# A decoder block on one core: cross attention scores from joined key halves, and maxima added by one product per bank

## The chip, the cores and the metric

The program runs on one core of one Trainium2 chip. The metric is the device time of one execution in microseconds (us). A core has five engines that run side by side, each with its own queue: PE (TensorE, matrix products into the eight PSUM banks), DVE (VectorE), ACT (ScalarE), POOL (GpSimd) and SP (SyncE, which here only issues DMAs). They wait for one another through semaphores. "PEld" in the profile is TensorE's loading of a stationary operand.

## The reference, cut to what matters

A decoder block over 64 sequences of 128 tokens, width 256, float32: a local attention, a cross attention on a second input (`ctx_1024`), and a slot network, each behind a layer norm and added to x. The change lies in the cross attention, 16 heads of 16:

```python
q = relu(query @ Wq + bq); k = relu(key @ Wk + bk); v = relu(value @ Wv + bv)
scores = einsum('bqhd,bkhd->bhqk', qh, kh) / sqrt(16)
scores = where(causal, scores, NEG)
probs = softmax(scores, axis=-1)
out = einsum('bhqk,bkhd->bqhd', probs, vh) + q
return layer_norm(out, gamma, beta)
```

## The kernel before, in words

Three stages follow one another: the local attention (to about 882 us of the profiled execution), the cross attention (882 to 1478 us) and the slot network. x stays in SBUF. A step works on a pair of sequences (`at`, 32 pairs); `tt` is the sequence in the pair. Each engine has its own program of steps in which `prev` is the pair one step behind, `old` two and `older` three; `pairs` (line 79) writes out the first and last steps and loops over the rest with two steps in a loop body. The order inside a step is written out by hand for each engine (`step`, TensorE's at line 1513), and no planner reorders it.

**Layout of the heads.** Queries and keys lie with the head dimension on the partitions: two projections (`e` = 0, 1) of 128 rows each. A row group `i` of 32 partitions (`group`, 1434) holds two heads, 16 rows each. To give each head its own product over 32 rows, `evac_k` (1567) writes the keys twice, once with the rows of one head made zero and once with the other's (`half`). A head's product has a stationary operand of 32 rows by 128 columns and a moving one of 32 rows by 128 columns; in float32 the trace shows two passes (two instructions) per product. The four row groups write the four score banks, group `i` bank `i`, and their products run beside one another. `slot(i, j)` is the j-th 128 columns of bank i.

**Per sequence**, TensorE does the following:
- `scores` (1440): 16 mask products (1453, bfloat16, 32x32 tiles, 512 columns), then 16 products query by key (1459) with the queries stationary, so that rows are queries. VectorE's `row_max` (1680) reduces all 16 heads at once, and `max_parts` (1684) splits the negated maximum into two bfloat16 parts and writes them to `max_part`, in 128 columns of which 32 are used.
- `max_transpose` (1464): one bfloat16 transpose of `max_part` into a bank; ScalarE's `copy_max` (1600) copies 128 columns to `max_t`.
- `scores_t` (1473): 16 products key by query (1482), keys stationary, so that rows are keys; after the four products of a `j` come four products (1485, bfloat16, 128 columns) with the stationary operand `pick` that add the negated maxima of slot (i, j). For tt = 1 the first product of a bank waits for ScalarE's exponential of that bank of tt = 0 (`exp_done`). The wait for `max_t` stands ahead of all of them.
- ScalarE's `exp` (1606), POOL's causal mask `mask_weights` (1786), and TensorE's `values` (1489), `back` (1503).

**Order around the change.** TensorE's step: scores(prev,0), back(old,0), values(old,1), project_k 0, scores(prev,1), max_transpose(prev,0), back(old,1), project_k 1, project_q 0, scores_t(prev,0), project_q 1, project_v 0, max_transpose(prev,1), scores_t(prev,1), project_v 1, transpose_q, transpose_x, values(prev,0), transpose_ctx. ScalarE's (1619): evac_av(old,1), copy_max(prev,0), evac_k, exp(prev,0), copy_max(prev,1), evac_q, exp(prev,1), copy_q_tok, relu_v, copy_xn, evac_av(prev,0), copy_ctx. VectorE's is at 1723, POOL's at 1810: mask_weights(old,1), scale_normed, add_query, mask_weights(prev,0), then the two pairs of reciprocal-deviation operations (`one_over_deviation`, 1774), which wait for VectorE's `sum_moments` and `x_moments`; these stand behind `bias_v` (1693), which waits for `project_v`.

Of the kernel before, what the change touches and what calls it, by code (L numbers as in the profile page):

```python
# [6 lines left out]
BF16 = mybir.dt.bfloat16  # L7
# [12 lines left out]
PT = 2 * S  # L20
# [138 lines left out]
class CrossWeights:  # L159


    def __init__(self, nc, scope):
        def sb(name, shape, dt=F32):
            return scope.enter_context(nc.sbuf_tensor(name, shape, dt))

        self.w_qk = sb("w_qk_b", [128, C, 4, 128])
        self.b_qk = sb("b_qk_b", [128, 4])
        self.w_v = sb("w_v_b", [128, C, D])
        self.b_v = sb("b_v_b", [128, D])
        self.gamma = sb("gamma", [128, D])  # L170
        self.beta = sb("beta", [128, D])
        self.mask = sb("mask_b", [128, 4, 128], BF16)
        self.row_half = sb("row_half", [128, 2])
        self.b_k = sb("b_k_half", [128, 2, 2])
        self.pick_f = sb("pick_f", [128, 4])
        self.pick = sb("pick", [128, 4, 128], BF16)
        self.minus_half = sb("minus_half", [128, 2])
        self.eps = sb("eps", [128, 2])


def attentions(nc, scope, sem, a, bank, x_sb, ident, ident_bf, cross):
# [87 lines left out]
    with nc.Block() as block:  # L269
# [39 lines left out]
        def _(dve):  # L309
# [25 lines left out]
            for w, g, products in terms:  # L335
# [9 lines left out]
            nc.vector.tensor_reduce(cross.pick_f[:],  # L345
                                    ident[:].rearrange("p (i u j) -> p j u i", i=4, j=4)[:, :, 0:2, :], AX.XY,
                                    ALU.add).then_inc(cross_made, 1)
# [8 lines left out]
            nc.vector.tensor_copy(cross.pick[:], cross.pick_f[:].unsqueeze(2).to_broadcast([128, 4, 128])  # L356
                                  ).then_inc(cross_made, 1)
            dve.wait_ge(cross_made, 5)
# [932 lines left out]
def cross_attention(nc, scope, sem, a, score_banks, bank, x_sb, ident, ident_bf, cross, slot_weights):  # L1291
# [6 lines left out]

    def sb(name, shape, dt=F32):
        return scope.enter_context(nc.sbuf_tensor("c_" + name, shape, dt))  # L1300
# [17 lines left out]
    k_z = [[sb(f"k_z{i}_{half}", [128, 2, PT]) for half in range(2)] for i in range(2)]  # L1318
# [4 lines left out]
    max_part = sb("max_part", [128, 2, 128], BF16)  # L1323
    max_t = sb("max_t", [128, 2, 128], BF16)
# [37 lines left out]
    with nc.Block() as block:  # L1362
# [19 lines left out]
        def _(pe):  # L1382
# [57 lines left out]
            def scores(at, tt):  # L1440
                if tt == 0:
                    pe.wait_ge(q_ready, at.count(1, 1))
                    pe.wait_ge(k_ready, at.count(1, 1))
                else:
                    pe.wait_ge(max_done, at.count(2, 1))
                    pe.sem_inc(pe_turn, 1)
                for i in range(4):
                    if tt == 0:
                        wait(pe, exp_done, at.count(8, i - 3))
                        pe.sem_inc(pe_turn, 1)  # L1450
                    for c in range(4):
                        rows = group((i + c) % 4)
                        pe.matmul(score_banks[group(c), i, :].rearrange("p (j k) -> p j k", j=4), ident_bf[rows, rows],
                                  cross.mask[rows, c, :].unsqueeze(1).to_broadcast([32, 4, 128]),
                                  start=True, stop=False, skip_group_check=True)
                toks = slice(S * tt, S * tt + S)
                for j in range(4):
                    for i in range(4):
                        mm = pe.matmul(slot(i, j), q_f[at.par][group(i), j % 2, toks],  # L1459
                                       k_z[at.par][j // 2][group(i), j % 2, toks],  # L1460
                                       start=False, stop=(j == 3), skip_group_check=True)
                mm.then_inc(sc_filled, 1)

            def max_transpose(at, tt):
# [3 lines left out]
                else:  # L1468
                    pe.wait_ge(maxT_ready, at.count(2, 1))
                pe.transpose(maxT_bank[:].bitcast(BF16)[:, 0:128], max_part[:, tt, :],  # L1470
                             ident_bf[:]).then_inc(maxT_filled, 1)

            def scores_t(at, tt):
                if tt == 0:
                    pe.wait_ge(max_done, at.count(2, 2))
                pe.wait_ge(maxT_ready, at.count(2, tt + 1))
                toks = slice(S * tt, S * tt + S)
                for j in range(4):
                    for i in range(4):
                        if tt == 1 and j == 0:  # L1480
                            pe.wait_ge(exp_done, at.count(8, i + 1))
                        pe.matmul(slot(i, j), k_z[at.par][j // 2][group(i), j % 2, toks],  # L1482
                                  q_f[at.par][group(i), j % 2, toks], start=True, stop=False, skip_group_check=True)
                    for i in range(4):
                        mm = pe.matmul(slot(i, j), cross.pick[group(i), j, :], max_t[group(i), tt, :],  # L1485
                                       start=False, stop=True, skip_group_check=True)
                mm.then_inc(sct_filled, 1)

            def values(at, tt):
# [5 lines left out]
                for h in range(H):  # L1495
                    g, j = h // 4, h % 4
                    if j == 0:
                        pe.wait_ge(masked, at.count(8, 4 * tt + g + 1))
                    mm = pe.matmul(av_bank[HW * j:HW * j + HW, 128 * g:128 * g + 128], v_heads[at.par][:, tt, h, :],  # L1499
                                   probs_t[tt][:, h, :], start=True, stop=True, skip_group_check=True)  # L1500
# [53 lines left out]
        def _(act):  # L1554
# [12 lines left out]
            def evac_k(at):  # L1567
                act.wait_ge(k_filled, at.count(2, 2))
                wait(act, sct_filled, at.count(2, -2))
                for half in range(2):  # L1570
                    for e in range(2):
                        ins = nc.scalar.activation(k_z[at.par][half][:, e, :], k_bank[:, e * PT:e * PT + PT], ACT.Relu,  # L1572
# [27 lines left out]
            def copy_max(at, tt):  # L1600
                act.wait_ge(maxT_filled, at.count(2, tt + 1))
                wait(act, sct_filled, at.count(2, tt - 1))
                nc.scalar.activation(max_t[:, tt, :], maxT_bank[:].bitcast(BF16)[:, 0:128],  # L1603
# [45 lines left out]
        def _(dve):  # L1649
# [34 lines left out]
            def max_parts(at, tt):  # L1684
                dve.wait_ge(max_done, at.count(2, tt + 1))
                wait(dve, maxT_filled, at.count(2, tt - 1))
                parts = max_part[:, tt, :].rearrange("p (i u j) -> p u i j", i=4, j=4)
# [704 lines left out]
```

## Time and profile before

| | us |
|---|---|
| median of 3 runs | 1788.61 (1787.81 to 1790.47) |
| the profiled execution's own time | 1789.42 |
| its span, first to last instruction | 1787.0 |
| cross attention in it | about 882 to 1478 |
| TensorE busy, whole span | 1612.1 (90%) |
| VectorE, ScalarE, POOL busy | 1367.5 (77%), 967.2 (54%), 946.1 (53%) |

The profiled execution took 2.42 us more than its span and lies 0.81 us above the median. Busy TensorE time counts from an instruction's start to a modelled end, so neighbours overlap: for throughput, read the distance between starts, not the durations. A row's "[0.44 <-ACT c_max_t L1603]" says that the engine stood idle 0.44 us before it and which instruction released it.

### The profile page before, as it was taken

To read this page: it belongs to the slowest core of one execution; us is meant where nothing else is said; L and a number is where in the kernel's file an instruction comes from. 1 tells how busy PE (TensorE), PEld (TensorE's weight loads), DVE (VectorE), ACT (ScalarE), POOL (GpSimd) and SP (SyncE) were. 2 spreads that over 40 slices of the span, in tenths; PEclk is the share of its full clock that TensorE was granted. 3 is DMA by queue.
4 is the path that set the end of the run, shared out by engine and by line. 5 is a ranking of instruction groups with operands and counts; after the bars stand their busy time and mean duration, and the time that the engine had idled before them with its cause. 6 is when DMAs were issued, how large, how long until landed. Compare 5 with 4: busy or idle time off the path is not lost. (4 is left out here: it accounts for less than half of the span.)

```text
span 1787.0 us, 52814 instructions
## 1 busy us (share of the span) xinstructions
PE 1612.1 (90%) x18272; PEld 1162.9 (65%) x18334; DVE 1367.5 (77%) x3280; ACT 967.2 (54%) x2049; POOL 946.1 (53%) x1205
## 2 busy tenths in 40 slices
PE   2799999999999999999699999999999976999997
PEld 1566666666666666666477777777777754666664
DVE  4688898989898989898356666666666644898996
ACT  1355555554555555555256565656565633777774
POOL 2345454545555555554336666666666662445544
PEclk9899999999999999999799999999999976999998
DMA  5554455545554455444210000000000000001001
GB/s 102 81 85 87 84 84 84 88 82 83 84 90 82 80 85 91 82 73 80 72 45 14 18 12 18 12 18 12 18 12 18 7 2 1 25 30 35 29 29 41
DMA packets 124323, 92.64 MB, mean 52 GB/s; under 512 B 34849, under 2 KB 122850, under 8 KB 124258
## 3 DMA queue, kind: packets, MB, share of 16 engines
q1 hardware_dynamic: 124258, 91.80, 28.1%
q8 instruction: 38, 0.62, 0.2%
q14 instruction: 27, 0.22, 0.1%
HBM read 23.06 MB, written 8.39 MB: 18 GB/s over the span
## 5 line engine op out<-in xcount | busy, mean ns | idle before, releaser
L1205 POOL TENSOR_SCALAR_AFFINE_SELECT probs_t<-probs_t 128x512 f32<-128x512 f32 x256 | 186.5, 743 | 220.7 <-ACT probs_t L894 220.6
L1682 DVE TENSOR_REDUCE c_neg_max<-score_banks 128x16 f32<-128x2048 f32 x64 | 146.5, 2290 | 100.4 <-PE score_banks L1459 100.3
L1610 ACT ACTIVATE c_probs_t<-score_banks 128x512 f32<-128x512 f32 x256 | 132.2, 603 | 66.0 <-PE score_banks L1485 66.0
L1791 POOL TENSOR_SCALAR_AFFINE_SELECT c_probs_t<-c_probs_t 128x512 f32<-128x512 f32 x256 | 155.4, 643 | 11.8 <-ACT c_probs_t L1610 11.7
L564 PE MATMUL score_banks<-xn_t,w_qk_a 128*128 128x256 f32 x512 | 133.7, 395 | 0.7 <-ACT xn_t L803 0.7
L1482 PE MATMUL score_banks<-c_q_f,c_k_z 32*128 32x128 f32 x2048 | 106.4, 307 | 22.0 <-ACT c_max_t L1603 15.4
L1482 PEld LDWEIGHTS score_banks<-c_q_f,c_k_z 32*128 32x128 f32 x2048 | 92.1, 188 | 45.3 <-ACT c_probs_t L1610 20.1
L713 PE MATMUL bank<-probs_t,v_heads 128*32 128x128 f32 x2048 | 109.2, 285 | 2.7 <-POOL probs_t L1205 0.8
L1042 DVE TENSOR_REDUCE neg_max<-score_banks 128x4 f32<-128x512 f32 x128 | 87.6, 684 | 21.3 <-PE score_banks L625 21.2
L894 ACT ACTIVATE probs_t<-bank 128x512 f32<-128x512 f32 x128 | 76.1, 595 | 41.4 <-PE bank L700 41.3
L564 PEld LDWEIGHTS score_banks<-xn_t,w_qk_a 128*128 128x128 f32 x512 | 91.6, 194 | 10.0 <-ACT xn_t L803 1.1
L1802 POOL TENSOR_TENSOR c_scaled<-c_normed,gamma 128x512 f32<-128x512 f32 x32 | 40.7, 1271 | 97.2 <-DVE c_normed L1665 97.2
L894 ACT ACTIVATE probs_t<-score_banks 128x512 f32<-128x512 f32 x128 | 76.1, 594 | 26.1 <-PE score_banks L700 25.9
L1042 DVE TENSOR_REDUCE neg_max<-bank 128x4 f32<-128x512 f32 x128 | 87.7, 685 | 2.6 <-PE bank L625 1.0
L1696 DVE TENSOR_TENSOR c_v_raw<-bank,b_v_b 128x512 f32<-128x512 f32 x32 | 22.1, 691 | 87.8 <-PE bank L1421 77.9
L2294 POOL TENSOR_TENSOR r_hn<-rz_t,half_hn 128x256 f32<-128x256 f32 x32 | 23.4, 731 | 124.0 <-ACT rz_t L2126 124.0
L2063 PE MATMUL bank<-w_ih,gi_t 128*128 128x512 f32 (+1 forms) x256 | 88.4, 488 | 0.4 <-DVE n_in L2229 0.2
L599 PE MATMUL score_banks<-w_v_a,xn_t 128*128 128x336 f32 x256 | 87.4, 464 | 0.3 <-ACT lat_raw L848 0.3
L1616 ACT ACTIVATE c_av_t<-bank 128x512 f32<-128x512 f32 x64 | 40.0, 625 | 77.7 <-PE bank L1499 77.7
L1572 ACT ACTIVATE c_k_z<-bank,b_k_half,row_half 128x256 f32<-128x256 f32 x128 | 61.9, 564 | 33.1 <-PE bank L1403 33.1
L1016 DVE TENSOR_TENSOR qk_rest<-qk_f,qk_part 128x512 f32<-128x512 f32 x64 | 74.9, 1170 | 6.1 <-ACT qk_f L829 6.1
L1499 PE MATMUL bank<-c_probs_t,c_v_heads 128*32 128x128 f32 x2048 | 74.4, 281 | 2.5 <-POOL c_probs_t L1791 1.8
(266 smaller groups left out, 4692.9 us busy)
## 6 DMA issues: line engine op xcount, KB each, us to landing
q_stack<-qk_part SPq DMA_DIRECT2D x192, 128.0 KB, 3.5
k_stack<-qk_part SPq DMA_DIRECT2D x192, 128.0 KB, 4.6
c_ctx_in<-in_ctx SPq DMA_DIRECT2D x32, 256.0 KB, 2.7
out<-y SPq DMA_DIRECT2D x32, 256.0 KB, 2.1
x_sb<-in_x SPq DMA_DIRECT2D x30, 256.0 KB, 2.7
rq_stack<-lat_part SPq DMA_DIRECT2D x192, 32.0 KB, 2.3
rk_stack<-lat_part SPq DMA_DIRECT2D x192, 16.0 KB, 1.9
w_ih<-in_ffn_w_ih SPq DMA_DIRECT2D x1, 768.0 KB, 5.8
```

The lines of the kernel that those rows point to most:

```text
L564: mm = pe.matmul(dst, w(c), src[:, c, :], start=(c == 0), stop=(c == C - 1))
L599: mm = pe.matmul(v_bank[tt][:, 0:n], src[:, c, S * tt:S * tt + S], w_v[:, c, :], start=(c == 0), stop=(c == C - 1))
L713: mm = pe.matmul(av_bank[HW * j:HW * j + HW, 128 * (g % 4):128 * (g % 4) + 128], v_heads[at.par][:, tt, h0 + j, :], probs_t[g % 4][:, j, : ...
L894: nc.scalar.activation(probs_t[g % 4][:].rearrange("p j t -> p (j t)"), score_bank[g % 2][:], ACT.Exp, scale=SCALE).then_inc(exp_done, 1)
L1016: nc.vector.tensor_tensor(rest, src, part[0], ALU.subtract).then_inc(part_step, 1)
L1042: nc.vector.tensor_reduce(neg_max[:, tt, h0:h0 + 4], score_bank[g % 2][:].rearrange("p (j k) -> p j k", k=128), AX.X, ALU.max, negate=True ...
L1205: nc.gpsimd.affine_select(out=pt[:], in_=pt[:], pattern=[[0, 4], [1, 128]], compare_op=ALU.is_ge, fill=0.0, base=-1 if local else 0, chann ...
L1482: pe.matmul(slot(i, j), k_z[at.par][j // 2][group(i), j % 2, toks], q_f[at.par][group(i), j % 2, toks], start=True, stop=False, skip_group ...
L1610: nc.scalar.activation(probs_t[tt][:, 4 * g:4 * g + 4, :].rearrange("p j q -> p (j q)"), score_banks[:, g, :], ACT.Exp, scale=SCALE).then_ ...
L1682: nc.vector.tensor_reduce(neg_max[:, tt, :], all_scores, AX.X, ALU.max, negate=True).then_inc(max_done, 1)
L1791: nc.gpsimd.affine_select(out=heads, in_=heads, pattern=[[0, 4], [1, 128]], compare_op=ALU.is_ge, fill=0.0, base=0, channel_multiplier=-1) ...
L2063: mm = pe.matmul(gate_bank[b][:, 0:hi - lo], gi_t[:, c, :], w.w_ih[:, c, lo:hi], start=(c == 0), stop=(c == C - 1))
```

## The change

The keys of both halves move into one tile, `k_z[par][:, e, half, :]`. In `scores`, one product with the same stationary query block takes both halves as a moving operand of 256 columns (two stretches of 128), 8 products in place of 16. This makes slot (i, j) hold e = j // 2 and half = j % 2, where it was the other way round; `scores_t` and `values` follow (`slot_j`). `max_parts` spreads the parts over four blocks of 128 columns, one per slot; `max_transpose` transposes four blocks in place of one, and `copy_max` copies 512 columns. In `scores_t` the 16 products key by query come first, without the pick products between; then comes the wait for `max_t`, and one product of 512 columns per bank against a tile of ones adds the maxima of its four heads, 4 products in place of 16. `pick` and `pick_f` go, `ones` comes.

```diff
-        self.pick_f = sb("pick_f", [128, 4])
-        self.pick = sb("pick", [128, 4, 128], BF16)
+        self.ones = sb("ones_b", [128, 128], BF16)
...
-            nc.vector.tensor_reduce(cross.pick_f[:],
-                                    ident[:].rearrange("p (i u j) -> p j u i", i=4, j=4)[:, :, 0:2, :], AX.XY,
-                                    ALU.add).then_inc(cross_made, 1)
+            nc.vector.memset(cross.ones[:], 1.0).then_inc(cross_made, 1)
...
-            nc.vector.tensor_copy(cross.pick[:], cross.pick_f[:].unsqueeze(2).to_broadcast([128, 4, 128])
-                                  ).then_inc(cross_made, 1)
-            dve.wait_ge(cross_made, 5)
+            dve.wait_ge(cross_made, 4)
...
-    k_z = [[sb(f"k_z{i}_{half}", [128, 2, PT]) for half in range(2)] for i in range(2)]
+    k_z = [sb(f"k_z{i}", [128, 2, 2, PT]) for i in range(2)]
...
-    max_part = sb("max_part", [128, 2, 128], BF16)
-    max_t = sb("max_t", [128, 2, 128], BF16)
+    max_part = sb("max_part", [128, 2, 4, 128], BF16)
+    max_t = sb("max_t", [128, 2, 512], BF16)
...
-                for j in range(4):
+                for e in range(2):
                     for i in range(4):
-                        mm = pe.matmul(slot(i, j), q_f[at.par][group(i), j % 2, toks],
-                                       k_z[at.par][j // 2][group(i), j % 2, toks],
-                                       start=False, stop=(j == 3), skip_group_check=True)
+                        mm = pe.matmul(score_banks[:, i, 256 * e:256 * e + 256].rearrange("p (s k) -> p s k", s=2),
+                                       q_f[at.par][group(i), e, toks], k_z[at.par][group(i), e, :, toks],
+                                       start=False, stop=(e == 1), skip_group_check=True)
                 mm.then_inc(sc_filled, 1)
...
-                pe.transpose(maxT_bank[:].bitcast(BF16)[:, 0:128], max_part[:, tt, :],
-                             ident_bf[:]).then_inc(maxT_filled, 1)
+                for j in range(4):
+                    mm = pe.transpose(maxT_bank[:].bitcast(BF16)[:, 128 * j:128 * j + 128], max_part[:, tt, j, :],
+                                      ident_bf[:])
+                mm.then_inc(maxT_filled, 1)
...
-                pe.wait_ge(maxT_ready, at.count(2, tt + 1))
                 toks = slice(S * tt, S * tt + S)
                 for j in range(4):
                     for i in range(4):
                         if tt == 1 and j == 0:
                             pe.wait_ge(exp_done, at.count(8, i + 1))
-                        pe.matmul(slot(i, j), k_z[at.par][j // 2][group(i), j % 2, toks],
-                                  q_f[at.par][group(i), j % 2, toks], start=True, stop=False, skip_group_check=True)
-                    for i in range(4):
-                        mm = pe.matmul(slot(i, j), cross.pick[group(i), j, :], max_t[group(i), tt, :],
-                                       start=False, stop=True, skip_group_check=True)
+                        pe.matmul(slot(i, j), k_z[at.par][group(i), j // 2, j % 2, toks],
+                                  q_f[at.par][group(i), j // 2, toks], start=(j == 0), stop=False, skip_group_check=True)
+                pe.wait_ge(maxT_ready, at.count(2, tt + 1))
+                for i in range(4):
+                    mm = pe.matmul(score_banks[:, i, :], cross.ones[group(i), :], max_t[group(i), tt, :],
+                                   start=False, stop=True, skip_group_check=True)
                 mm.then_inc(sct_filled, 1)
...
-                                   probs_t[tt][:, h, :], start=True, stop=True, skip_group_check=True)
+                                   probs_t[tt][:, 4 * g + slot_j, :], start=True, stop=True, skip_group_check=True)
...
-                nc.scalar.activation(max_t[:, tt, :], maxT_bank[:].bitcast(BF16)[:, 0:128],
+                nc.scalar.activation(max_t[:, tt, :], maxT_bank[:].bitcast(BF16)[:, 0:512],
                                      ACT.Copy).then_inc(maxT_ready, 1)
...
-                parts = max_part[:, tt, :].rearrange("p (i u j) -> p u i j", i=4, j=4)
+                parts = max_part[:, tt, :, :].rearrange("p j (i u) -> p u i j", i=4)
```

## Rows read from the trace of the kernel before

**Rows 1.** The page: TensorE's busy time, its share of the span, instructions.

```profile
PE 1612.1 (90%) x18272; PEld 1162.9 (65%) x18334; DVE 1367.5 (77%) x3280; ACT 967.2 (54%) x2049; POOL 946.1 (53%) x1205
```

**Rows 2.** Busy time by engine over 29 steady steps (x: instructions).

```profile
936.00:1451.00 515.00, 495.33 (x8778) 386.76 (x8778) 335.81 (x717) 300.19 (x665) 335.13 (x460) 1.00 0.05 14
```

**Rows 3.** Line 1682, the row maxima: durations, first and last start.

```profile
L1682 DVE TENSOR_REDUCE c_neg_max<-score_banks x64: 2280/2292/2293, 898.8 to 1451.4; 128x16 f32<-128x2048 f32 x64
```

**Rows 4.** Waits, 930 to 1470 us: total us, times, longest us.

```profile
PEld score_banks L1482 <- ACT c_probs_t L1610: 20.1, 26, 0.8
...
PE score_banks L1482 <- ACT c_max_t L1603: 14.7, 30, 2.1
...
PEld bank L1499 <- POOL c_probs_t L1791: 7.0, 17, 0.4
```

**Rows 5.** Timeline of one step: start, length (us), engine, line [idle before].

```profile
1203.01 1.17 PE L1459 MATMUL score_banks<-c_k_z,c_q_f 32*128 32x128 f32 x32
...
1204.12 0.23 PE L1470 MATMUL bank<-ident_bf,c_max_part 128*128 128x128 bf16 x1
...
1204.41 2.28 DVE L1682 TENSOR_REDUCE c_neg_max<-score_banks 128x16 f32<-128x2048 f32 x1
...
1204.62 1.03 PE L1403 MATMUL bank<-c_ctx_t,w_qk_b 128*128 128x256 f32 x4
...
1205.49 1.03 PE L1403 MATMUL bank<-c_xn_t,w_qk_b 128*128 128x256 f32 x4
...
1206.75 0.50 PE L1482 MATMUL score_banks<-c_q_f,c_k_z 32*128 32x128 f32 x8 [0.23 <-DVE c_neg_max L1682]
...
1207.07 0.23 PE L1485 MATMUL score_banks<-c_max_t,pick 32*128 32x128 bf16 x4
...
1207.13 0.46 PE L1482 MATMUL score_banks<-c_q_f,c_k_z 32*128 32x128 f32 x8
...
1207.40 0.23 PE L1485 MATMUL score_banks<-c_max_t,pick 32*128 32x128 bf16 x4
...
1208.07 0.23 PE L1485 MATMUL score_banks<-c_max_t,pick 32*128 32x128 bf16 x4
...
1210.07 0.22 PE L1470 MATMUL bank<-ident_bf,c_max_part 128*128 128x128 bf16 x1
1210.32 0.28 ACT L1603 ACTIVATE c_max_t<-bank 128x128 bf16<-128x128 bf16 x1
...
1210.73 0.70 PE L1482 MATMUL score_banks<-c_q_f,c_k_z 32*128 32x128 f32 x6 [0.44 <-ACT c_max_t L1603]
...
1212.38 0.21 PE L1485 MATMUL score_banks<-c_max_t,pick 32*128 32x128 bf16 x1
...
1212.63 2.07 ACT L1610 ACTIVATE c_probs_t<-score_banks 128x512 f32<-128x512 f32 x4 [1.30 <-PE score_banks L1485]
...
1213.49 0.60 PE L1430 MATMUL bank<-ident,c_q_f 128*128 128x128 f32 x4
...
1213.93 0.60 PE L1388 MATMUL bank<-ident,c_xn 128*128 128x128 f32 x4
...
1216.67 2.40 POOL L1791 TENSOR_SCALAR_AFFINE_SELECT c_probs_t<-c_probs_t 128x512 f32<-128x512 f32 x4
```

**Rows 6.** Groups by line and form, 900 to 1500 us: busy us, mean ns | idle.

```profile
L1616 ACT ACTIVATE c_av_t<-bank 128x512 f32<-128x512 f32 x64 | 40.0, 625 | 77.7 <-PE bank L1499 77.7
...
L1453 PE MATMUL score_banks<-mask_b,ident_bf 32*32 32x512 bf16 x1008 | 32.1, 384 | 2.0 <-DVE c_neg_max L1682 2.0
...
L1603 ACT ACTIVATE c_max_t<-bank 128x128 bf16<-128x128 bf16 x64 | 17.8, 278 | 68.2 <-PE bank L1470 68.2
```

**Rows 7.** Timeline of the start of the cross attention.

```profile
884.31 0.17 DVE L1756 MEMSET c_max_part<- 128x128 uint32 x1
...
885.39 1.09 PE L1397 MATMUL bank<-ident,c_ctx_in 128*128 128x128 f32 x4 [4.33 <-DMA c_ctx_in<-in_ctx]
```

**Rows 8.** Timeline of vector engine's first work after the set-up block.

```profile
26.39 0.75 DVE L985 BATCH_NORM_STATS2 stats<-x_sb 128x6 f32<-128x256 f32 x2 [7.27 <-PEq L269]
```

More of the change, by code:

```diff
@@ L1496, in values @@
                     g, j = h // 4, h % 4
+                    slot_j = 2 * (j % 2) + j // 2
                     if j == 0:
@@ L1571, in evac_k @@
                     for e in range(2):
-                        ins = nc.scalar.activation(k_z[at.par][half][:, e, :], k_bank[:, e * PT:e * PT + PT], ACT.Relu,
+                        ins = nc.scalar.activation(k_z[at.par][:, e, half, :], k_bank[:, e * PT:e * PT + PT], ACT.Relu,
                                                    bias=cross.b_k[:, half, e:e + 1],
```

## The prediction

> **What bounds the kernel now.** I read the page first, then the busy time by engine of the cross attention, then its waits, then one step of the timeline. The page shows TensorE busy 90% of the span [rows 1]. The change touches only the cross attention, so its own table counts: over 29 steady steps of 515.0 us, 17.76 us a step, TensorE is busy 495.3 us, VectorE 335.8, POOL 335.1, ScalarE 300.2, at full granted clock (1.00, 2.4 GHz) [rows 2]. TensorE is the bound, with 0.68 us idle a step. The row maxima show how long the stage lasts: first start 898.8, last 1451.4, 64 of them [rows 3], for 32 steps.
>
> The waits say where the idle time lies: TensorE's products of `scores_t` wait 14.7 us, 30 times, about 0.5 us a step, for `max_t` (tt = 1; its weight loads, ahead of it, wait 20.1 us for the exponentials of tt = 0); POOL's mask holds `values` back 7.0 us in all, 17 times [rows 4]. The timeline shows the rest. `row_max` of tt = 1 runs from 1204.41 to 1206.69 while TensorE does transposes and two projections, and `scores_t` of tt = 0 starts at 1206.75 after 0.23 us of idle time; so that stretch is nearly balanced between VectorE and TensorE. `scores_t` of tt = 1 starts at 1210.73 after the 0.44 us wait, and lasts until 1212.59; `exp` follows at 1212.63 [rows 5]. A step's period is thus a path that is TensorE nearly everywhere, with short stretches handed to `row_max`, `exp` plus `copy_max`, and POOL.
>
> A difference within 0.2% (3.6 us) is about what a measurement of this kernel can't tell from none.
>
> **The change part by part**, per step of two sequences.
>
> *Joined key halves in `scores`.* Before, 32 passes of 128 columns take from 1203.01 to the next operation's start at 1204.12, 1.11 us; that is 8 passes in each of four row groups that run side by side, 0.139 us a pass. A pass of 256 columns over the whole array takes (1205.49 - 1204.62) / 4 = 0.218 us [rows 5], so doubling the columns costs less than double: some of the 128-column pass is the exchange of the stationary operand. After, 4 passes of 256 columns per row group are 0.87 us, and 0.97 if the 0.1 us of changing over to the next operation is in the 1.11. I take a saving of 0.14 us per sequence, with ends 0 (cost goes by columns) and 0.24. For tt = 1 it counts in full: `row_max` starts at its end. For tt = 0, TensorE next meets `values(old,1)`, which already waits for POOL in 17 of 30 steps [rows 4]; POOL's mask (1216.67, 2.40 us [rows 5]) follows from `project_v` through VectorE's and POOL's small operations and doesn't move with `scores`. I take 0.05.
>
> The Trainium skill (TensorE: Matmul & The Clock Gate, "Back-to-back issue gap") gives N / 2.4 + 2.5 ns between warm products of N columns: by that rule joining two halves saves nearly nothing. It speaks against this part; the 0.139 against 0.218 us above do not follow it. By the rule this term would be about 0, and it is the first rival below.
>
> *`max_transpose`, four transposes in place of one.* Nearest row: float32 transposes over the whole array, four in 1213.93 - 1213.49 = 0.44 us, 0.11 each; a lone bfloat16 one lasts 0.22 or 0.23 [rows 5]. Three more cost 0.33 us (ends: 0 and 3 x 0.23 = 0.69). For tt = 0 they lie under `row_max`, where TensorE idles 0.23 us, so 0.10 comes out. If that cover were gone, 0.33. For tt = 1 see below.
>
> *`copy_max`, 512 columns.* 278 ns now; ScalarE's other copies of 512 columns take 625 [rows 6]: 0.35 us more. For tt = 0 ScalarE idled before it (68.2 us in 32 steps [rows 6]), and the result is needed only at the end of `scores_t`: 0. Behind it in ScalarE's queue is `evac_k`, which waits for the projection anyway. For tt = 1 it runs right behind `exp` of tt = 0, from about 1210.3 or when the transposes end (1210.6), to about 1211.2, before the ones products need it at about 1211.6. Queued behind are `evac_q` (0.83 us, unchanged) and `exp` of tt = 1, which had 1.30 us of idle time [rows 5]. So 0; if the cover went, 0.35.
>
> *The wait for `max_t` moved behind the 16 products.* For tt = 1 the products start once the transposes are issued and the exponentials are done (about 1210.3): 1210.07 + 0.11 + 0.33 = 1210.51 in place of 1210.73, 0.22 us gained. The transposes eat half of the freed wait.
>
> *`scores_t` itself.* For tt = 0 it takes 1206.75 to 1208.30, 1.55 us: each j costs 0.33 (1207.07 to 1207.40), of which 0.27 for the eight passes and 0.06 for the start of four pick products [rows 5]. After: 4 x 0.27 = 1.08 for the passes, then four products of 512 columns in four row groups and four banks. The mask products, 512 columns and bfloat16, last 384 ns each [rows 6] and sixteen of them overlap; so 1.46 us, 0.09 saved. Ends: 0.2 saved, or the slower rival below. For tt = 1 it lasts 1.86 us, 0.31 more than for tt = 0, since the four row groups start one after another and the picks keep them out of step; I take a third of that, so 0.19 in all.
>
> *Set-up, layout.* The reduce and the cast for `pick` go, but VectorE next waits 7.27 us for the end of the block [rows 8]: 0. The memset of `max_part` is four times as large, 0.17 us to at most 0.7; TensorE's first transposes wait for a DMA until 885.39 [rows 7], the memset ends 0.9 us before: 0. VectorE's two 16-element writes of `max_parts`, the evacuation of keys and `values` keep their shapes: 0.
>
> **The sum**: 0.05 + 0.14 - 0.10 + 0.22 + 0.09 + 0.19 = 0.59 us a step, 32 steps, 18.9 us. The profiled execution took 1789.4, so 1770.5; it lies 0.8 above the median, so 1770 is forecast against 1788.6.
>
> **The rivals.**
> 1. *Cost goes by columns.* `scores` and `scores_t` save nothing; what is left is the moved wait (0.22), some of the staggered start (0.10), less 0.10: 0.22 a step, 7 us, 1781.6. For it: no row has a 256-column product in a row group of 32, nor one whose moving operand is in two stretches. Against: 0.139 and 0.218. 15%.
> 2. *More comes back.* Passes at the short end (0.24), `scores_t` 0.2 shorter for each sequence and no stagger: about 0.9 to 1.0 a step, 30 us, 1759. Against: VectorE's and POOL's chains then hold TensorE. 15%.
> 3. *Another engine takes the gain.* POOL's masks or `row_max` bind in every step rather than in half of them: both `scores` terms go and the transposes come out dearer, 0.3 a step, 1779. For: waits of 0.23 and 7.0 us exist already. Against: POOL's chain starts at `project_v`, which itself moves earlier with `scores_t`. 12%.
> 4. *Slower: the ones products don't overlap.* They sit at the end of `scores_t`, where `exp` waits for all of them. If the four banks are written one after another, at 0.218 us for 512 bfloat16 columns (taken equal to the 256-column float32 pass), three more are 0.65 us per sequence, 1.3 a step, all on the path: 0.59 becomes -0.71, 23 us slower, 1811. It decides from 0.3 us of extra time per sequence. For: the trace has no four products of 512 columns that each write all 128 partitions. Against: four picks start within 0.06 us. 6%.
> 5. *Slower: transposes that don't overlap.* At 0.69 us for three, tt = 0 pays 0.46 and tt = 1 loses 0.25 in place of gaining 0.22: -0.24 a step, 8 us, 1796. 4%. The Trainium skill (same page, "Part 4: PE-mode transpose") has about 275 ns for such a transpose in a kernel; here the float32 ones follow at 0.11.
>
> **How the numbers follow.** The forecast's case has 46% (1764 to 1776); the last 2% are that it does nothing. Faster by over 0.2%: the forecast, rivals 1, 2 and most of 3, 0.83. Within 0.2%: 0.07, from the weak ends of rivals 1 and 3. Slower: rivals 4 and 5, 0.10. The range takes rivals 2, 1 and 3 whole or nearly, 1757 to 1785, and leaves the two slower ones out.
>
> **What would show it right or wrong.** In the profile after: 1024 passes of line 1459's successor with 256 columns (half as many), from first start to next operation about 0.97 us; four transposes within some 0.55 us; no wait for `max_t` ahead of the first products of `scores_t` and none worth naming ahead of the ones products; `exp` of tt = 1 about 0.6 us earlier against the step's start; more waiting of `values` on POOL; a step of about 17.2 us. Wrong would be ones products whose starts lie 0.2 us apart, a `scores` still 1.1 us long, or a new TensorE wait for ScalarE's longer copy.

## The result, and the profile after

The changed kernel takes 1756.62 us (median of 4 runs, 1755.95 to 1757.63) beside 1788.75 us for the kernel before; the ratio is 0.982, with a 95% interval of 0.9803 to 0.9837. That is 32.1 us faster, where 18.9 were forecast; 1756.62 lies just under the low end of the range, 1757. The profiled execution took 1757.11 us, with a span of 1755.4. One execution of `c3_wait_moved` ran at a granted clock of 0.868 in place of 0.97 and took 1812.49 us; it is left out of every comparison.

The page's row for TensorE [rows 1] is now:

```profile
PE 1598.6 (91%) x16672; PEld 1131.7 (64%) x16734; DVE 1377.1 (78%) x3279; ACT 990.7 (56%) x2049; POOL 945.4 (54%) x1205
```

1600 instructions fewer, but 13.5 us less busy time only. The row maxima [rows 3] now read:

```profile
L1681 DVE TENSOR_REDUCE c_neg_max<-score_banks x64: 2280/2292/2293, 896.3 to 1421.9; 128x16 f32<-128x2048 f32 x64
```

Taking off the 4.3 us between the two sequences of a step, a step is (525.6 - 4.3) / 31 = 16.82 us, where it was (552.6 - 4.3) / 31 = 17.69: 0.87 us less, 28 us over 32 steps. Between the two profiled executions, 32.3 us apart, 27.0 (552.6 - 525.6) lie between the first and the last row maximum. The first starts at 896.3 in place of 898.8, and from the last to the end of the span it is 333.5 us in place of 335.6. So 2.5 and 2.1 us were gained ahead of and behind the stage that the change was meant to touch, and 0.7 outside the span.

The waits of the same stage [rows 4], total us, times, longest:

```profile
ACT c_probs_t L1609 <- PE score_banks L1483: 14.9, 31, 3.0
PEld score_banks L1479 <- DVE c_neg_max L1681: 14.0, 30, 2.0
...
PEld bank L1498 <- POOL c_probs_t L1790: 7.2, 17, 0.4
```

The view names no wait of TensorE for `max_t` or for the exponentials any more; ScalarE, which waited for `scores_t` 62.7 us before, waits 14.9. POOL holds `values` back as often as before (7.2 us, 17 times). The timeline of one step, to be laid beside [rows 5] (1455 was 1459, 1467 was 1470, 1479 was 1482, 1483 was 1485, 1609 was 1610, 1790 was 1791):

```profile
1185.77 1.15 PE L1455 MATMUL score_banks<-c_k_z,c_q_f 32*128 32x256 f32 x16
...
1186.85 0.40 PE L1467 MATMUL bank<-ident_bf,c_max_part 128*128 128x128 bf16 x4
...
1187.08 0.61 PE L1509 MATMUL bank<-ident,c_av_t 128*128 128x128 f32 x4
1187.21 2.28 DVE L1681 TENSOR_REDUCE c_neg_max<-score_banks 128x16 f32<-128x2048 f32 x1
...
1189.55 1.17 PE L1479 MATMUL score_banks<-c_q_f,c_k_z 32*128 32x128 f32 x32
...
1190.54 0.39 PE L1483 MATMUL score_banks<-c_max_t,ones_b 32*128 32x512 bf16 x4
...
1192.70 0.39 PE L1467 MATMUL bank<-ident_bf,c_max_part 128*128 128x128 bf16 x4
...
1193.01 1.24 PE L1479 MATMUL score_banks<-c_q_f,c_k_z 32*128 32x128 f32 x32
1193.12 0.60 ACT L1602 ACTIVATE c_max_t<-bank 128x512 bf16<-128x512 bf16 x1
...
1194.01 0.46 PE L1483 MATMUL score_banks<-c_max_t,ones_b 32*128 32x512 bf16 x4
...
1194.50 2.07 ACT L1609 ACTIVATE c_probs_t<-score_banks 128x512 f32<-128x512 f32 x4
...
1198.54 2.40 POOL L1790 TENSOR_SCALAR_AFFINE_SELECT c_probs_t<-c_probs_t 128x512 f32<-128x512 f32 x4
...
1200.99 0.43 PE L1498 MATMUL bank<-c_probs_t,c_v_heads 128*32 128x128 f32 x8 [0.16 <-POOL c_probs_t L1790]
```

Measured from the start of `row_max` of tt = 1, line by line against [rows 5]:

| stretch | before | after | saved |
|---|---|---|---|
| `row_max` to `scores_t` of tt = 0 | 2.34 | 2.34 | 0 |
| from there to `scores_t` of tt = 1 | 3.98 | 3.46 | 0.52 |
| from there to `exp` of tt = 1 | 1.90 | 1.49 | 0.41 |
| from there to POOL's mask of tt = 1 | 4.04 | 4.04 | 0 |

So 0.93 us of this step went, all of it between two points: the starts of `scores_t` of tt = 0 and of `exp` of tt = 1. The first and last steps gain less, which makes the mean 0.87. The transposes are cheap: four and the start of what follows take 1187.08 - 1186.85 = 0.23 us. `scores` takes 1.08 us to the next operation with half the products, and took 1.11.

### The profile page after: what moved, and what is told of

Its sections match the earlier page's. It is cut to its first block and busy times, and to the rows that moved or that the text cites. A ratio compares the mean times of both kernels' runs of the same rounds, so it can differ in the third digit from the quotient of the medians.

```text
span 1755.4 us, 49575 instructions
## 1 busy us (share of the span) xinstructions
PE 1598.6 (91%) x16672; PEld 1131.7 (64%) x16734; DVE 1377.1 (78%) x3279; ACT 990.7 (56%) x2049; POOL 945.4 (54%) x1205
## 5 line engine op out<-in xcount | busy, mean ns | idle before, releaser
L1479 PE MATMUL score_banks<-c_q_f,c_k_z 32*128 32x128 f32 x2048 | 79.1, 285 | 3.6 <-DVE c_neg_max L1681 2.1
L1602 ACT ACTIVATE c_max_t<-bank 128x512 bf16<-128x512 bf16 x64 | 38.2, 598 | 75.1 <-PE bank L1467 72.7
L1479 PEld LDWEIGHTS score_banks<-c_q_f,c_k_z 32*128 32x128 f32 x2048 | 66.8, 188 | 18.5 <-DVE c_neg_max L1681 15.1
```

The costliest lines, as they stand in the source:

```text
L1479: pe.matmul(slot(i, j), k_z[at.par][group(i), j // 2, j % 2, toks], q_f[at.par][group(i), j // 2, toks], start=(j == 0), stop=False, skip_ ...
```

## The experiments

All times are medians. They were taken in three groups, with the kernel before beside each: 1787.38 us beside `a1`, `a2`, `b1` and `b2`; 1788.08 beside `c3`, `c4`, `c5` and `d1_pad`; 1787.46 beside `c1`, `d2`, `e1` and `f1`. The changed kernel itself was run again only in the third group (`f1_changed_again`, 1755.91 us).

The whole time also holds what happens outside the cross attention, and that scatters by some us. The row maxima measure the stage alone, in each profiled execution, first start to last start of the 64:

| run | first | last | us between |
|---|---|---|---|
| before | 898.8 | 1451.4 | 552.6 |
| `b2_one_wait` | 899.4 | 1443.3 | 543.9 |
| `c3_wait_moved` | 897.4 | 1433.3 | 535.9 |
| `b1_picks_last` | 897.4 | 1423.3 | 525.9 |
| changed, and again (`f1`) | 896.3, 895.1 | 1421.9, 1420.5 | 525.6, 525.4 |
| padded (`d1`), and again (`d2`) | 900.0, 897.0 | 1425.4, 1422.7 | 525.4, 525.7 |
| `a1_unjoined` | 896.3 | 1422.6 | 526.3 |
| `a2_wait_first` | 896.0 | 1453.4 | 557.4 |
| `c1_one_wait_after` | 896.5 | 1422.8 | 526.3 |
| `c4_twice_tt0` | 893.0 | 1422.8 | 529.8 |
| `c5_twice_tt1` | 895.2 | 1425.8 | 530.6 |
| `e1_pool_order` | 894.0 | 1414.0 | 520.0 |

**Join undone** (changed kernel, `a1_unjoined`): 1755.64 us, ratio to before 0.9826 (0.9813 to 0.984).

```diff
-                for e in range(2):
+                for j in range(4):
                     for i in range(4):
-                        mm = pe.matmul(score_banks[:, i, 256 * e:256 * e + 256]..., q_f[at.par][group(i), e, toks],
-                                       k_z[at.par][group(i), e, :, toks], ...)
+                        mm = pe.matmul(slot(i, j), q_f[at.par][group(i), j // 2, toks],
+                                       k_z[at.par][group(i), j // 2, j % 2, toks], ...)
```

> The changed kernel with 16 products of 128 columns in scores again, all else as changed. Theory A (the join is worth nearly nothing: start of scores to the next operation is 1.08 us after and 1.11 before, 0.03 us per sequence): 1 to 2 us slower than the changed kernel, about 1758. Theory B (the forecast's, 0.05 to 0.14 us per sequence on the path): 6 us slower, about 1763.

The timeline of `scores` in it, 32 passes again, and the operation behind:

```profile
1186.19 1.17 PE L1455 MATMUL score_banks<-c_k_z,c_q_f 32*128 32x128 f32 x32
...
1187.30 0.40 PE L1467 MATMUL bank<-ident_bf,c_max_part 128*128 128x128 bf16 x4
```

1.11 us against 1.08 with the join, and no slower overall; the stage takes 526.3 us in place of 525.6. The join is worth less than 1 us; theory B falls.

**The wait put back** (changed kernel, `a2_wait_first`): 1787.52 us, ratio to before 1.0001 (0.9992 to 1.001).

```diff
+                pe.wait_ge(maxT_ready, at.count(2, tt + 1))
                 toks = slice(S * tt, S * tt + S)
 ...
-                pe.wait_ge(maxT_ready, at.count(2, tt + 1))
                 for i in range(4):
                     mm = pe.matmul(score_banks[:, i, :], cross.ones[group(i), :], max_t[group(i), tt, :], ...
```

> The changed kernel with the wait for max_t ahead of the 16 products key by query again. Theory A (the moved wait is most of the gain; the transposes end at 1193.1 and the copy of 512 columns takes 0.60, so the products of tt = 1 start about 0.8 us later): 25 us slower than the changed kernel, about 1782. Theory B (the start is set by the exponentials, the wait costs what it did, 0.3 us): 10 us slower, about 1767.

```profile
1188.51 1.17 PE L1480 MATMUL score_banks<-c_q_f,c_k_z 32*128 32x128 f32 x32
...
1191.66 0.39 PE L1467 MATMUL bank<-ident_bf,c_max_part 128*128 128x128 bf16 x4
...
1192.08 0.60 ACT L1602 ACTIVATE c_max_t<-bank 128x512 bf16<-128x512 bf16 x1
...
1192.81 1.38 PE L1480 MATMUL score_banks<-c_q_f,c_k_z 32*128 32x128 f32 x31 [0.76 <-ACT c_max_t L1602]
```

With this one line in its old place the whole gain is gone. `copy_max` is now 0.60 us long and TensorE waits 0.76 us for it; `scores_t` of tt = 1 starts 4.30 us after that of tt = 0, against 3.46. Both theories said too little: A by 5 us. Its last row shows 31 passes over 1.38 us, where the changed kernel has 32 over 1.24: the row groups are also further out of step. The stage takes 557.4 us, 4.8 more than before; the whole time comes out equal because this kernel keeps what the changed one gains outside the stage.

**Only the order of scores_t** (kernel before, `b1_picks_last`): 1760.32 us, ratio 0.9849 (0.9833 to 0.9864).

```diff
-                pe.wait_ge(maxT_ready, at.count(2, tt + 1))
 ...
                         pe.matmul(slot(i, j), k_z[...], q_f[...], start=(j == 0), stop=False, ...)
+                pe.wait_ge(maxT_ready, at.count(2, tt + 1))
+                for j in range(4):
                     for i in range(4):
                         mm = pe.matmul(slot(i, j), cross.pick[group(i), j, :], max_t[group(i), tt, :], ...)
```

> The kernel before, with only the order of scores_t changed: 16 products key by query, then the wait for max_t, then the 16 pick products; one transpose, a copy of 128 columns, no join. Theory A (order and wait carry the gain): 1755 to 1760, as fast as the changed kernel or slightly faster, since three transposes a sequence are saved. Theory B (fewer, wider products carry it): only the 0.44 us wait goes, about 1775.

Both sequences in it (1481 the products, 1486 the picks, 1611 `exp`):

```profile
1190.81 1.17 PE L1481 MATMUL score_banks<-c_q_f,c_k_z 32*128 32x128 f32 x32 [0.23 <-DVE c_neg_max L1683]
...
1191.81 0.40 PE L1486 MATMUL score_banks<-c_max_t,pick 32*128 32x128 bf16 x16
...
1194.12 1.29 PE L1481 MATMUL score_banks<-c_q_f,c_k_z 32*128 32x128 f32 x31
...
1195.14 0.28 PE L1486 MATMUL score_banks<-c_max_t,pick 32*128 32x128 bf16 x6
...
1195.26 0.49 PE L1486 MATMUL score_banks<-c_max_t,pick 32*128 32x128 bf16 x10
...
1195.78 2.07 ACT L1611 ACTIVATE c_probs_t<-score_banks 128x512 f32<-128x512 f32 x4 [0.55 <-PE score_banks L1486]
```

Theory A: with none of the wide products, the join or the copies of 512 columns, 27 of the 32 us are there. The products of tt = 1 start 3.31 us after those of tt = 0; the changed kernel takes 3.46, since its transposes stand in between. In return `exp` follows 1.66 us after the start, against 1.49 in the changed kernel. That is not the price of 16 picks against four ones products: for tt = 0 `exp` follows `scores_t` by 1.44 us here and by 1.43 there. It is the earlier start. The fourth row group has to wait for the last exponential of tt = 0, and starts 0.25 us after the first here, 0.08 us after it there. The two cancel.

**One wait for the exponentials** (kernel before, `b2_one_wait`): 1779.88 us, ratio 0.9952 (0.9938 to 0.9965).

```diff
+                if tt == 1:
+                    pe.wait_ge(exp_done, at.count(8, 4))
 ...
-                        if tt == 1 and j == 0:
-                            pe.wait_ge(exp_done, at.count(8, i + 1))
```

> The kernel before, with one wait for all four exponentials ahead of scores_t of tt = 1 in place of one wait per bank. Theory A (the four waits between the first products set the row groups out of step, which is the 0.31 us by which tt = 1 is longer): up to 10 us faster than before, about 1779. Theory B (the weight loads ahead of the max_t wait, or the pick products between, do it): unchanged, 1788.

```profile
1185.14 0.50 PE L1482 MATMUL score_banks<-c_q_f,c_k_z 32*128 32x128 f32 x8
...
1189.12 0.50 PE L1482 MATMUL score_banks<-c_q_f,c_k_z 32*128 32x128 f32 x8 [0.44 <-ACT c_max_t L1603]
...
1190.44 0.24 PE L1485 MATMUL score_banks<-c_max_t,pick 32*128 32x128 bf16 x4
...
1190.72 2.07 ACT L1610 ACTIVATE c_probs_t<-score_banks 128x512 f32<-128x512 f32 x4 [1.00 <-PE score_banks L1485]
```

`scores_t` of tt = 1 begins 3.98 us after that of tt = 0, exactly as before, but `exp` follows after 1.60 us instead of 1.90. So the 0.31 us that the prediction saw between the two sequences comes from the four waits that stand between the first four products. 7.5 us in all, 8.7 in the stage. The products of tt = 1 that began by 1210.84 in the kernel before and by 1189.14 in this one:

```profile
1210.73 0.48 PE L1482 MATMUL score_banks<-c_q_f,c_k_z 32*128 32x128 f32 x2 [0.44 <-ACT c_max_t L1603]
```

```profile
1189.12 0.39 PE L1482 MATMUL score_banks<-c_q_f,c_k_z 32*128 32x128 f32 x3 [0.44 <-ACT c_max_t L1603]
```

Before, the four row groups start 0.11 us apart, 0.34 us from first to fourth; here 0.007 us apart. No exponential held them up: in the step of [rows 5] the last one ended at 1210.42, 0.31 us before the first product. The four waits were long satisfied and still set the groups 0.11 us apart. In these runs they do so only right behind the wait for `max_t`, which has just held the queue. In the changed kernel the same four waits stand there, but the wait for `max_t` does not, and the first three groups start within 0.014 us; in `a2_wait_first`, where it stands there again, they are 0.11 us apart again. The picks between the groups are not what keeps them out of step: `a2_wait_first` has none there, and its `exp` of tt = 1 follows 1.75 us after the start against 1.43 for tt = 0, the same 0.32 us.

**Only the wait** (kernel before, `c3_wait_moved`): 1770.30 us, ratio 0.9902 (0.9887 to 0.9917).

```diff
-                pe.wait_ge(maxT_ready, at.count(2, tt + 1))
 ...
                     for i in range(4):
                         if tt == 1 and j == 0: ...
                         pe.matmul(slot(i, j), k_z[...], q_f[...], start=True, ...)
+                    if j == 0:
+                        pe.wait_ge(maxT_ready, at.count(2, tt + 1))
                     for i in range(4):
                         mm = pe.matmul(slot(i, j), cross.pick[group(i), j, :], ...
```

> The kernel before, with the wait for max_t moved behind the first four products key by query and nothing else; picks stay between the groups. Theory A (the moved wait has a gain of its own; with picks last, the products of tt = 1 began 3.31 us after those of tt = 0, against 3.98 before): the start moves by 0.4 to 0.6 us, 13 to 19 us off, 1768 to 1774. Theory B (wait and order work only together, since the row groups out of step give back what the earlier start wins): 5 us off or less, above 1782.

```profile
1196.41 0.50 PE L1481 MATMUL score_banks<-c_q_f,c_k_z 32*128 32x128 f32 x8 [0.23 <-DVE c_neg_max L1683]
...
1199.87 0.62 PE L1481 MATMUL score_banks<-c_q_f,c_k_z 32*128 32x128 f32 x7
...
1201.70 2.07 ACT L1611 ACTIVATE c_probs_t<-score_banks 128x512 f32<-128x512 f32 x4 [0.71 <-PE score_banks L1486]
```

The start comes 3.46 us after tt = 0 in place of 3.98, 0.52 us, and 17.8 us in all: theory A. The wait cost more than the 0.44 us that its row [rows 5] showed, because that idle time counts from the modelled end of the transpose, 0.22 us after its start; without the wait the products start 0.15 us after it. From the start to `exp` it is 1.83 us in place of 1.90: three row groups now start within 0.014 us, and the fourth, 0.25 us later, waits for the last exponential itself. The 10 us between this kernel and `b1_picks_last` (535.9 to 525.9 in the stage) are the order: with the picks behind all products, `scores_t` to `exp` is 0.16 us shorter for each sequence (1.60 to 1.44 and 1.83 to 1.66).

**Transposes twice**, for tt = 0 (`c4_twice_tt0`) and for tt = 1 (`c5_twice_tt1`), in the changed kernel.

```diff
-                for j in range(4):
+                for j in [0, 1, 2, 3] * (2 if tt == 0 else 1):
                     mm = pe.transpose(...)
```

> The changed kernel with the four transposes of tt = 0 done twice (the same values written again). Theory A (a transpose costs 0.057 us and those of tt = 0 lie under row_max, behind which TensorE idles about 0.3 us): 0 to 2 us slower than the changed kernel, 1756 to 1759. Theory B (the forecast's cover of 0.23 us is used up by the first three): 7 us slower, 1764.

> The changed kernel with the four transposes of tt = 1 done twice. Theory A (those of tt = 1 lie on TensorE's own path, 4 x 0.057 us a step): 7 us slower than the changed kernel, 1764. Theory B (the exponentials of tt = 0 cover them): 1 us or less, 1757. By the forecast's price of 0.11 us each it would be 14 us, 1771.

For tt = 0: 1760.70 us, 1755.68 to 1762.73. The profiled execution is the fastest of the four, since it reached the cross attention early (first row maximum at 893.0); its stage takes 529.8 us, 4.2 more than the changed kernel's. Two steps one after the other (transposes, `row_max`, products):

```profile
1185.87 0.62 PE L1467 MATMUL bank<-ident_bf,c_max_part 128*128 128x128 bf16 x8
1186.24 2.28 DVE L1681 TENSOR_REDUCE c_neg_max<-score_banks 128x16 f32<-128x2048 f32 x1
...
1188.59 1.17 PE L1479 MATMUL score_banks<-c_q_f,c_k_z 32*128 32x128 f32 x32
...
1202.91 0.62 PE L1467 MATMUL bank<-ident_bf,c_max_part 128*128 128x128 bf16 x8
1203.05 2.29 DVE L1681 TENSOR_REDUCE c_neg_max<-score_banks 128x16 f32<-128x2048 f32 x1 [0.26 <-PE score_banks L1455]
...
1205.63 1.17 PE L1479 MATMUL score_banks<-c_q_f,c_k_z 32*128 32x128 f32 x32
```

Eight start and end within 0.62 us. In the first step `scores_t` begins 2.35 us after `row_max` (2.34 in the changed kernel), in the second 2.58 us. In both they begin 2.72 us after the transposes; what differs is how late `row_max` starts. So `row_max` covers them in one step of two and not in the other, and its cover has an end just there; neither theory held whole. For tt = 1: 1759.65 us (1759.09 to 1760.77).

```profile
1191.20 1.17 PE L1479 MATMUL score_banks<-c_q_f,c_k_z 32*128 32x128 f32 x32
...
1194.35 0.61 PE L1467 MATMUL bank<-ident_bf,c_max_part 128*128 128x128 bf16 x8
...
1194.89 1.17 PE L1479 MATMUL score_banks<-c_q_f,c_k_z 32*128 32x128 f32 x32
...
1196.32 2.07 ACT L1609 ACTIVATE c_probs_t<-score_banks 128x512 f32<-128x512 f32 x4
```

The products begin 3.69 us after those of tt = 0, the full 4 x 0.057 us later than 3.46, as theory A has it; but by then all exponentials are done, the four waits hold nothing up, and `exp` comes 1.43 us after the start in place of 1.49. By these rows 0.17 us a step, 5 us, and that is what the stage shows (530.6 against 525.6); the whole time is 3 to 4 us longer (1759.65 against 1756.62 and 1755.91). Both lie between the theories.

**An unused tile** (changed kernel, `d1_pad` and `d2_pad_again`; the changed kernel itself once more, `f1_changed_again`).

```diff
         self.ones = sb("ones_b", [128, 128], BF16)
+        self.pad = sb("pad", [128, 196])
```

> The changed kernel with an unused tile of 784 bytes a partition beside the ones, so that all later tiles of SBUF lie where they lay before. The local attention, which the change leaves alone, ended 3.3 us earlier after it. Theory A (the places of its tiles do that): the cross attention starts at about 882 us again and the time is 3 us longer, 1760. Theory B (scatter between executions): it starts at about 879 to 880, time unchanged, 1756 to 1757.

> The changed kernel itself, beside the padded one on the same chip. If the places of the tiles matter (theory A), it is 3 to 4 us faster than the padded one, 1756 to 1757, and its local attention ends near 879 us; if the difference was scatter (theory B), the two agree within 1 us.

> The padded kernel once more. Theory A: 1760, local attention to 882 or 883 us. Theory B: as the changed kernel beside it.

1760.21 (1759.38 to 1762.01) and, beside 1755.91 us (1754.13 to 1757.84) for the changed kernel on the same chip, 1761.51 (1759.85 to 1762.40). Without touching an instruction of any stage, 784 bytes of padding cost 4 to 6 us. The padding puts the tiles of the local attention and of the slot network back where they lay, but not all of the cross attention's: `max_part` and `max_t` are 1536 bytes larger each than before, and what lies behind them stays moved. The table of the stages says where the time goes: not into the cross attention (525.4 and 525.7 us padded, 525.6 and 525.4 not). Over all profiled executions, the first row maximum comes at 897.0 to 900.0 us in the six kernels with the old places (before, both padded, and the three built on the kernel before) and at 893.0 to 896.5 in the eight with the new ones, 3.0 us earlier on average; behind the last one the mean is 2.7 us shorter, though there the two sets overlap. `d2_pad_again` did not meet its theory A in one point: its local attention ended at about 880 us, not 882 or 883, against 878 for the changed kernel beside it.

TensorE's wait for the transposed maxima of the local attention, 100 to 850 us, in the kernel before, in `f1_changed_again` and in `d2_pad_again`:

```profile
PEld score_banks L700 <- DMA q_stack<-max_t: 12.9, 26, 0.7
```

```profile
PEld score_banks L695 <- DMA q_stack<-max_t: 10.7, 26, 0.5
```

```profile
PEld score_banks L696 <- DMA q_stack<-max_t: 12.8, 26, 0.7
```

In all six profiled executions with the old places this wait is 12.8 to 14.5 us, in all eight with the new ones 10.7 to 11.3. Theory A, then; that is 2 of the 4 to 6 us. What about the places does it is open: only one distance was tried, 784 bytes, and no run tells which tile matters.

**One wait, after** (changed kernel, `c1_one_wait_after`, the edit of `b2_one_wait`): 1756.28 us (1755.94 to 1756.57).

> The changed kernel with one wait for all four exponentials ahead of scores_t of tt = 1. Theory A (in the changed kernel the four waits cost only 0.07 us, since 1.39 us from its start to the next operation stand against 1.32 for tt = 0, and one wait gives that back by starting about 0.1 us later): unchanged within 2 us. Theory B (the four waits still cost what they did before the change): 7 us faster, 1749.

As theory A has it: in the changed kernel the four waits cost next to nothing. With one wait in their place all four groups start in step and `exp` follows after 1.43 us in place of 1.49, but the start comes 3.55 us after tt = 0 in place of 3.46.

**POOL's order** (changed kernel, `e1_pool_order`): 1748.63 us, ratio 0.978 (0.9766 to 0.9793), the shortest time of all these kernels.

```diff
-                prev, old, older, second = at.back(), at.back(2), at.back(3), at.back(-2)
+                prev, old, older, following = at.back(), at.back(2), at.back(3), at.back(-1)
                 if old.real:
                     mask_weights(old, 1)
+                if older.real:
+                    out_deviation(older)
+                if following.real and (not isinstance(at.i, int) or at.off >= 1):
+                    x_deviation(following)
 ...
                 if prev.real:
                     mask_weights(prev, 0)
-                if old.real:
-                    out_deviation(old)
-                if second.real:
-                    x_deviation(second)
```

> The changed kernel with POOL's two reciprocal-deviation pairs moved behind mask_weights of tt = 1. Theory A (values waits for POOL's masks in half of the steps, 0.4 us each, and TensorE bounds everything else): 6 us faster than the changed kernel, about 1750. Theory B (the idle time moves to the next wait, row_max or the exponentials): 2 us or less, 1755 to 1757.

```profile
1187.41 4.96 POOL L1790 TENSOR_SCALAR_AFFINE_SELECT c_probs_t<-c_probs_t 128x512 f32<-128x512 f32 x8
...
1192.35 0.20 POOL L1775 TENSOR_TENSOR c_out_var_eps<-c_out_moments,eps 128x2 f32<-128x2 f32 x1
...
1194.67 1.08 PE L1498 MATMUL bank<-c_probs_t,c_v_heads 128*32 128x128 f32 x32
```

POOL's eight masks now run in one piece and end at 1192.37, before `values` of tt = 1 starts at 1194.67 and runs its 32 products without a stop. The waits of this kernel, 930 to 1440 us, name none of `values` for POOL's masks any more, and the stage takes 520.0 us, 5.4 less than the changed kernel beside it; the whole time is 7.3 us shorter. Theory A holds.

## Why the prediction was wrong

The lead of the mechanism was right: faster, through `scores_t`, with the moved wait worth most; and TensorE stays the bound. A third of the forecast sum, the join, was wrong, and the size was off by 13 us, in several terms. A step, in us:

| term | forecast | measured |
|---|---|---|
| joined key halves | 0.05 + 0.14 | 0 to 0.03 |
| transposes of tt = 0 | -0.10 | 0 |
| moved wait, less the transposes of tt = 1 | 0.22 | 0.35 |
| `scores_t` of tt = 0 | 0.09 | 0.17 |
| `scores_t` of tt = 1 | 0.19 | 0.41 |
| sum | 0.59 | 0.93 to 0.96 |

The steps of the prediction that failed:

- *Joined key halves.* The step that failed is the reading of 1.11 us as eight passes of 0.139 each, against 0.218 for 256 columns. That spreads the start and the end of the block, about 0.2 us, over the passes (0.1 was allowed for at one end). In the traces, passes of one row group start 0.112 us apart with 128 columns and 0.216 us apart with 256, apart from the first; so twice the columns cost nearly twice, and half the passes still need 1.08 us. A `scores` "still 1.1 us long" was one of the prediction's own signs of being wrong, and it came. The rule of the Trainium skill (TensorE: Matmul & The Clock Gate, "Back-to-back issue gap"), N / 2.4 + 2.5 ns, by which cost goes by columns, was the better guide to this part: the measured ratio is 1.93, the rule's 1.96. The prediction gave it 15%.
- *Transposes*, 0.11 us each from float32 ones: 0.057 measured for bfloat16. Those of tt = 0 cost 0 in place of 0.10, under the cover of `row_max`; `c4_twice_tt0` shows that the cover ends just behind them.
- *The moved wait*, 0.22 us forecast, 0.35 measured. The wait itself was sized about right: without the three added transposes the prediction's working gives 1210.73 - 1210.18 = 0.55 us, and `c3_wait_moved` shows 0.52. What failed is again the price of the transposes, 0.33 us in place of 0.17.
- *scores_t*, 0.28 us forecast for both sequences, 0.58 measured, the largest miss. Half of it is the price of the 32 passes, 4 x 0.27 = 1.08 us, where they take 0.99 (1189.55 to 1190.54), once for each sequence. The other half is the 0.31 us by which tt = 1 was longer. The prediction named the row groups that start one after another, and took a third of it without a reason; 0.24 came back. It also held that the picks keep the groups out of step, and `a2_wait_first` shows the same 0.32 us without them. `b2_one_wait` puts the 0.30 us on the four waits, and the moved wait takes most of that away.
- *Set-up and layout*, 0 forecast: the prediction counted instructions and not the 784 bytes by which later tiles move, worth 4 to 6 us outside the cross attention. No row of the trace of before could show it.

The cover of `copy_max` held for both sequences: for tt = 1 it ends 0.29 us before the ones products at 1194.01 would need it. More waiting of `values` on POOL was forecast and did not come (17 times before and after).

Of the rivals, the first (cost by columns) was right about the join and wrong about the sum, since it held that `scores_t` saves nothing. The second had nearly the size (1759): its `scores_t` was close, 0.2 for each sequence and no stagger, but its 0.24 for the join was wrong, and that it still came near the time is luck, since it did not count the 4 to 6 us of the tile places. The third was half right: POOL does bind in the same steps as before, and 7.3 us were to be had there, but it did not eat the gain. The two slower ones fell: four ones products start and end within 0.39 us, and four transposes and the start of the next operation take 0.23.

In one line, by the stage: moving the wait 17 us, moving the picks behind all products 10 us; outside the stage, tile places 4 to 6 us. The wider products, the joined keys and the larger transposes and copies together come to nothing: the padded kernel, which has them all (525.4 and 525.7 us in the stage, 1760.2 and 1761.5 in all), and the one that has none of them (`b1_picks_last`, 525.9 and 1760.3) are equal.

## What to carry to other kernels

Put a wait directly ahead of the first instruction that needs it, and put the work that doesn't need it in front: on TensorE's queue that was worth 1% here, where fewer and wider products were worth nothing. Several waits behind one that has just held the queue can cost time even when all of them are satisfied; where a group of products on separate row groups starts with one wait per group, compare it with the same group without such waits. Price a pass by the distance between starts inside a block, not by the block's length over the number of passes. And compare a change that moves memory with a padded twin before small differences are explained.

## What was not expected of the hardware

Sixteen float32 passes of 256 columns in four row groups take 1.08 us, 32 of 128 columns 1.11. Four full bfloat16 transposes start 0.057 us apart, float32 ones 0.11. Four satisfied waits between the first products of four row groups set them 0.11 us apart behind a wait that held the queue (`before`, `a2_wait_first`), and 0.007 us apart for the first three where none had (the changed kernel). An unused tile of 784 bytes changed the time outside the only stage that was edited: 1755.9 against 1761.5 us, with the stage itself at 525.4 and 525.7 us.
